# New orders of instructions on all engines of a cross-attention kernel

## The reference

```python
# x, ctx: (32, 512, 512); 16 heads of 32
qn = layer_norm(x, q_norm_g, q_norm_b)
kvn = layer_norm(ctx, kv_norm_g, kv_norm_b)
Q, K, V = split_heads(qn @ Wq), split_heads(kvn @ Wk), split_heads(kvn @ Wv)
attn = softmax(Q @ K.T / sqrt(32))
out = x + gelu(merge_heads(attn @ V) @ Wo + bo)   # exact gelu
```

## Time and profile before

| | us |
|---|---|
| median of 3 runs | 3232.85 |
| lowest, highest | 3230.54, 3233.08 |
| the profiled execution, its own time | 3231.49 |
| its span | 3229.7 |
| PE busy | 3196.3 (99%) |
| PE weight loads | 2148.0 (67%) |
| DVE busy | 2274.2 (70%) |
| ACT busy | 2306.6 (71%) |
| POOL busy | 2318.6 (72%) |

### The profile page before, as it was taken

One profiled execution on the slowest core, in us unless ns is written; L12 is line 12 of the kernel. 1 busy time (PEld: TensorE's weight loads), 2 busy tenths in 40 slices (PEclk: granted clock), 3 DMA queues, 4 the chain that ended last, 5 costly groups with the idle time before them and its releaser, 6 DMA issues.

```text
span 3229.7 us, 50112 instructions
## 1 busy us (share of the span) xinstructions
PE 3196.3 (99%) x16611; PEld 2148.0 (67%) x16611; DVE 2274.2 (70%) x4769; ACT 2306.6 (71%) x3985; POOL 2318.6 (72%) x1544
## 2 busy tenths in 40 slices
PE   8999999999999999999999999999999999999998
PEld 5566666666666666666666666666666666666664
DVE  6677677677677776776776777766767767777664
ACT  4677767777767777677777677776777776777765
POOL 2677677777777777777777777777777777777775
PEclk9999999999999999999999999999999999999999
DMA  4445445345444354453454444544534544544442
GB/s 147 101 104 129 115 119 133 95 115 137 115 115 120 104 130 115 120 133 95 115 136 116 115 119 105 130 115 121 131 95 115 138 115 114 121 105 128 115 102 79
DMA packets 193010, 376.85 MB, mean 117 GB/s; under 512 B 22625, under 2 KB 22641, under 8 KB 188658
## 3 DMA queue, kind: packets, MB, share of 16 engines
q1 hardware_dynamic: 192288, 372.86, 45.2%
q10 hardware_dynamic: 466, 0.80, 0.1%
HBM read 138.42 MB, written 33.82 MB: 53 GB/s over the span
## 4 chain that ended last, share of the span: by engine, by line
PE 98%; DVE 1%; ACT 1%; issue 0%; DMA 0%; ACTq 0%; POOL 0%
PE gen L868 43%; PE score L896 15%; PE score L888 15%; PE ctx L916 15%; PE gen L859 4%; PE gen L956 3%; PE gen L978 1%; DVE maxes L718 1%; PE score L800 0%; ACT probs L575 0%; PE gen L849 0%; ACT q_stack L629 0%; PE score L849 0%; ACT tok L596 0%; PE score L827 0%
## 5 line engine op out<-in xcount | busy, mean ns | idle before, releaser
L487 POOL TENSOR_TENSOR probs<-probs 128x1024 f32<-128x1024 f32 x762 | 1806.5, 2405 | 430.1 <-PE ctx L916 426.2
L718 DVE TENSOR_REDUCE maxes<-score 128x1 f32<-128x512 f32 x2048 | 1304.0, 681 | 267.8 <-PE score L896 256.7
L575 ACT ACTIVATE probs<-score 128x512 f32<-128x512 f32 x2048 | 1083.5, 606 | 229.7 <-PE score L888 219.9
L896 PE MATMUL score<-k_stack,q_stack 128*128 128x512 f32 x2048 | 728.7, 404 | 0.8 <-DVE maxes L718 0.2
L888 PE MATMUL score<-q_stack,k_stack 128*128 128x512 f32 x2048 | 713.9, 401 | 6.4 <-ACT q_stack L629 5.1
L896 PEld LDWEIGHTS score<-k_stack,q_stack 128*128 128x128 f32 x2048 | 380.0, 188 | 216.2 <-issue 81.1
L888 PEld LDWEIGHTS score<-q_stack,k_stack 128*128 128x128 f32 x2048 | 377.8, 188 | 185.6 <-ACT probs L575 42.4
L916 PE MATMUL ctx<-probs,v_sb 128*32 128x512 f32 x4096 | 492.4, 598 | 0.6 <-ACT probs L575 0.5
L868 PE MATMUL gen<-cT,w_k 128*128 128x512 f32 x1536 | 451.9, 399 | 0.1
L868 PE MATMUL gen<-xT,w_q 128*128 128x512 f32 x1536 | 444.0, 395 | 0.0
L868 PE MATMUL gen<-w_v,cT 128*128 128x512 f32 x1536 | 443.8, 390 | 0.0
(11 more groups left out here) (89 smaller groups left out, 2720.9 us busy)
## 6 DMA issues: line engine op xcount, KB each, us to landing
k_stack<-k_nat SPq DMA_DIRECT2D x384, 256.0 KB, 4.2
q_stack<-q_nat SPq DMA_DIRECT2D x381, 256.0 KB, 5.1
tok<-in_x SPq DMA_DIRECT2D x132, 256.0 KB, 6.0
tok<-in_ctx SPq DMA_DIRECT2D x128, 256.0 KB, 6.3
q_stack<-zero_rows SPq DMA_DIRECT2D x128, 256.0 KB, 3.3
res<-in_x SPq DMA_DIRECT2D x124, 256.0 KB, 2.6
out<-res SPq DMA_DIRECT2D x124, 256.0 KB, 2.5
probs<-in_L_xattn_Wq SPq DMA_DIRECT2D x1, 1024.0 KB, 8.5
```

Of the source, the lines that this page charges most:

```text
L487: pool.tensor_tensor(probs[:, c + 1, heads], probs[:, c + 1, heads], probs[:, c, heads], ALU.add).then_inc(pool_added, 1)
L575: act.activation(probs[:, n, part, :], score_at(s, "st", i)[:], ACT.Exp, scale=SCALE).then_inc(exp_done, 1)
L718: dve.tensor_reduce(maxes[:, u1 % 2, SROW + i:SROW + i + 1], score_at(s, "s", i)[:], AX_X, ALU.max, negate=True).then_inc(max_done, 1)
L896: pe.matmul(score_bank(pe, b, s, "s", i)[:, :], q_stack[:, u1 % 2, n, P * part:P * (part + 1)], k_stack[:, u1 % 2, n, :], start=True, stop ...
```

## The change

Only the strings of `ORDER` are new. Each engine has the same items in a batch, in another order; a few items cross from one stage to another (on PE two parts of `o` leave stage 1, one for stage 0 and one for stage 2; on SP one `load`, the stores and residual loads), and code, costs and banks follow from the table by the same rules.

```diff
     "pe": (
-        "q*3 v*2 s q s q s v st*2 v st q st s st v st*2 v s v*2 st s st z s st*2 v st v*2 s*2 v st s pv st s "
...
+        "q*3 s q s v q s v s q s v st s st*2 q st*2 s v st*2 v st s st v st*2 s v st s z v s v st v s v*3 pv st s "
...
     "sp": (
...
-        "rk store rq rz first_res",
...
+        "first_res res rq rz rk store first_res",
     ),
```

More of the change, by code:

```diff
@@ L52 @@
     "pe": (
[8 rows of a table removed]
[8 rows of a table added]
     ),
     "act": (
[4 rows of a table removed]
[4 rows of a table added]
     ),
     "dve": (
-        "s ln s*2 ln s la ln q ln s la s la zt zr lv s zb lv*2 cn la s*9 md ml ln k ob",
-        "ln la lv la ln q lv zt zr zb ln la x s lv s cn lv s*2 k x s x la s lv x*2 s*4 x s*2 x ob s*2 x s*2 "
+        "s*5 ln s ln la lv s ln la s lv q s la zt zr s zb cn lv s*6 md ml k ob ln la",
+        "ln*2 lv ln q la zt la zr lv*2 zb x la s*2 cn lv s*2 x k x s ln s*2 x*2 la lv s*2 x s x s*3 ob s*3 x "
         "md ob ml",
-        "s*5 ob s*2 zt s zr zb s cn s*4 k s*3 md q ml",
-        "k zt zr zb cn s*2 q s*14 md ml",
+        "s*5 ob s*4 zt s zr zb s cn s*4 k s md ml q",
+        "k zt zr zb cn q s*16 md ml",
     ),
     "pool": (
-        "ln*3 split add*6 ln*3 res_add",
-        "ln add ln add*3 res_add add res_add add split",
+        "ln*3 split add*6 ln*2 res_add ln",
+        "ln add*2 ln add*3 res_add add res_add split",
         "add*6 split res_add",
-        "split add*6",
+        "add*5 split add",
     ),
     "sp": (
-        "load*6 rz rq load*2 rk store res",
-        "rz rq rk",
-        "store res rz rk rq store first_res",
-        "rk store rq rz first_res",
+        "load*5 rq load*2 rz rk",
+        "load store rz rq res rk",
+        "rk store*2 rq rz",
+        "first_res res rq rz rk store first_res",
     ),
```

## The result

| | before | after |
|---|---|---|
| median of 6 runs | 3231.69 | 3250.51 |
| lowest, highest | 3230.07, 3235.09 | 3247.47, 3251.44 |
| span of the profiled execution | 3229.7 | 3248.6 |
| before the first full batch | 162.5 | 170.7 |
| thirty full batches | 2959.7 (98.66 each) | 2966.6 (98.89 each) |

The ratio is 1.0056, 95% interval 1.0043 to 1.0069: the change makes the kernel slower, by 18.8 us in the medians. The forecast was no change, 3229.7, with a range that ended at 3244. The lower rows cut the two profiled executions at the `m` (transpose of the maxima) that opens the first full batch and at the one that closes the last.

A forecast was written before the change was run, and what follows sets the result against it. TensorE (PE), busy 2958.94 of 2959.8 us, was taken as the bound. Terms of -0.13 a batch over 31.5 batches gave -4.1, head +0.9, tail 0, together -3.2: median 3232.85 to 3229.7, range 3220 to 3244.

The forecast's parts named there:

- The part in the name: PE: score-after-score pairs fall from 64 to 59 a batch, each costing 0.00 to 0.01 more: -0.02 a batch.
- The switches: PE entries into and exits from narrow groups and transposes change little: 0 a batch, range -0.12 to +0.11.
- Waits that go: Per batch: stage 1 gelu bank -0.04, spreading activations -0.04, stage 3 `z` behind low `k` -0.14, small places -0.05.
- +0.9 (0 to 1.5): Prologue stage 3: eight `v` matmuls before the first score instead of four, so DVE's maxima start later: +0.9 in all.
- the rival of late loads: SP's store behind seven transfers delays tile loads, DVE stands at the statistics: up to 1.0 a batch, 3240 to 3261; chance 0.12.
- POOL is no term: POOL's six additions finish before PE reaches `z` in either order, so they add nothing to the sum.
- (a): End of stage 2: the second `pv` waits for all 16 exponentials: +0.10 a batch, range 0 to 0.2.
- (b): `mx` behind ACT's copy of `q` ends later, so the first `st` waits: +0.03 a batch.
- (c): Stage 1: four scores whose bank comes free within 0.05 of their turn: +0.03 a batch, range 0 to 0.3.
- (d): Stage 0: the product of the sums ends 0.05 before `pv` needs it: 0, range to +0.2.
- Small ties: Rival: (b) to (d) and the POOL cover all go against the forecast: +0.2 to +0.4 a batch, 3236 to 3242; chance 0.13.
- the POOL cover: Stage 0: POOL's split precedes the last addition, which ends 0.4 before `z`; if that failed, 0.3 a batch.

The follow-up runs named there:

- the losses repaired: The changed kernel with the eighth prologue load early, POOL's residual addition earlier, ACT's split behind all four `mx`, `q` restack before the stores: 3233.99, ratio 1.0007.
- the swap on PE: The changed kernel with those four edits, and in stage 3 one more part of `k` ahead of the first transposed score: 3231.23, ratio 0.9998.
- The two runs with this load: Eighth prologue tile load ahead of the weight loads in the changed kernel: 3245.08, ratio 1.0036; behind them in the kernel before: 3243.60, ratio 1.0034.
- the run with the early load: The changed kernel, in the prologue alone the eighth tile load issued ahead of the clearing store and four weight loads: 3245.08, ratio 1.0036.
- the run with `m` first: The changed kernel with four edits and the PE swap of `k`, last batch still with `m` before `pv` in stage 2: 3231.23, ratio 0.9998.
- the run with `pv` first: The run with four edits and the PE swap, plus `pv` before `m` at the end of stage 2 in the last batch alone: 3230.37, ratio 0.9997.

## Why the prediction was wrong

The forecast was -3.2 and the two medians are 18.8 apart, so 22 us are to be explained: some 7.3 in the head (+0.9 forecast, 8.2 measured), 10.8 in the thirty steady batches (-3.9 and +6.9) and 3.8 in the tail (0 and 3.8).

**The bound, right.** PE sets the pace. Over thirty batches its order decides by starts, not by busy time.

**The part in the name, right in direction, and zero.** The forecast took -0.02 a batch for five pairs. Averaged over thirty batches, places over 0.24 left out, a score ahead of a score has a distance of 0.230 to the next start in the trace of before (54 places), any other pair of these matmuls 0.228 to 0.2295; with the change 0.230 and 0.229 to 0.2295. Five pairs are at most 0.01 a batch. By the Trainium skill's rule ("TensorE: Matmul & The Clock Gate", section "Back-to-back issue gap"), which has no term for the neighbour, it is 0; on that the trace agrees.

**The switches, right.** Taken at 0, in a range of -0.12 to +0.11; by the distances into and out of narrow groups and transposes they came to +0.05.

**Waits that go, right.** The wait of the first token transpose for gelu is not among the waits of the change, `z` of stage 3 no longer meets the low part of `k`, `pv` stays 3.75 behind `z` and `m` 0.14 behind the copy. With the losses repaired the steady batch is 98.57, 0.09 under before, and 98.47 with the swap on PE; the forecast was 98.53.

**The head: a step that failed.** The term "+0.9 (0 to 1.5)" counted PE's and DVE's work in stage 3 of the prologue and nothing of SP. The moved `load` was seen, in the rival of late loads, but only in the steady batch, where it indeed costs nothing. That in the prologue other transfers stand between SP's stages was never looked at, though the code and the queue of before show it. The two runs with this load price it at 6.5 and 10.7 us. Without the head the change would have ended at about 3242, inside the range.

**"POOL is no term": wrong ground, and the second step that failed, a term missing.** That paragraph held POOL's additions against `z` alone, and there it was right. But `z` of stage 2 also needs a bank, and gelu of the last tile frees it. This term is not in the sum: 0.18 at `z`, 0.22 a batch in all, 6.6 us. The cause is not POOL either: with POOL's residual addition early the loss stayed, and with the split behind the four `mx` it went. The change moved the last part of the output projection into stage 2, the split waits for it, and on ACT one `mx` and the gelu stand behind the split. The forecast followed the moved bank (from `x` to `z`), and not the chain that frees it.

**(a) fits.** The second `pv` of stage 2 starts 0.21 behind `m` and 0.07 behind the last exponential (1331.45); the term of 0.10 can't be separated further. **(b) mis-sized:** +0.03 was 0.11 (and 4.08 against 4.03, its own working, is 0.05). The last spreading activation ends 3.97 behind `m` and the score starts 4.02 behind it, both as forecast; but the wait doesn't show in that start. It shows in the distance to the next, 0.33, which the sum had at 0.227. **(c) mis-sized:** some 0.1 instead of 0.03 in stage 1, within its range to 0.3. **(d) right:** 0.

**The restack of q, not foreseen.** The forecast followed the store and the loads to their new places in SP's queue, and not the restack of `q`, which the change put behind two stores: 0.08 a batch in stage 3, 0.14 by the run without it.

**The tail: 0, plus or minus 1, was +3.8.** About 1.7 lies ahead of `z` of stage 3 (82.4 behind the steady batches, 80.7 before): the first score of stage 2 waits 2.01 for the spreading activations, 0.17 before, the clock falls behind that wait, and POOL's additions start 1.9 later. Most of it is the clock: the run with the early load has the same code and the same 2.01 there, its clock stayed at 1.00 over 3186 to 3199, and its `z` came at 81.0. About 2.1 lies behind its start: 0.87 is the slow `z`, the rest the last four scores and their exponentials, which come behind it. The forecast had `m` before `pv` as a gain for ACT. It is one, and PE paid for it in front of `z`.

**The rivals.** Of the slower ones the late tile loads did not come (the loads were there in time). Small ties, 3236 to 3242, come nearest, but at half the measured loss: (b) and (c) had a part, (d) and the POOL cover had none in the steady batches, and it lacked the split, the restack, the head and the tail.

## What to carry to other kernels

An item that moves from one stage's list to the next must be followed in every copy of the loop. Prologue and last batch put other things between the lists, and one 256 KB load behind 4 MB of weights cost more than all that was to be won in thirty batches. A bank that changes hands needs the whole chain of its new releaser checked, to the engine's item in front of it and what that waits for. And a wait that the profile names is the one that came last: take it away and look at what stands right behind it before it is called the cause.

## What was not expected of the hardware

A wait of TensorE can cost more than its length where the work behind it is bound by TensorE. The clearest case is the run with the copy of `q` late: a stop of 2.6 in every batch, and behind it the granted clock at 0.50 in 21 of thirty, some 1.5 more each time. The tail shows the same. After 2.16 idle the granted clock was 0.66 over 3219 to 3224, and a group of `z` took 1.93 instead of 1.06; in the run with `m` first twelve products took 4.26 instead of 2.98. A longer idle time (3.42) ahead of scores that ACT paces was followed by a clock of 0.50 as well (3197.5 to 3200 in the kernel before, 3196 to 3202 in the run with `pv` first), but there it fell on work that waits for ACT anyway, and the products behind took 3.00 and 2.98. A wait is not the only thing ahead of a fall: in the kernel before the granted clock is 0.79 over 40 to 48 us, and PE had not waited from 20 to 40 (busy 20.00 of 20.00, clock 1.00). The head of one and the same prologue code varied by 4.5 us between executions, and the clock there differed with it (granted 0.67 and 1.00 over 40 to 50 us, first transpose of maxima at 72.0 and 67.4). How the single gains overlap (20.1 one by one, 15.8 together) and what the last 1.1 of the tail is was not settled.
